# Expert lists by counting and one-hot products, one program block, and expert weights asked for by two engines

## What is computed

```
x = x + attention(norm(x), ctx, ctx) @ w_out.T             # 16 heads, causal
x = x + ffn(norm(x))                                       # dense, 1376 wide, plus LoRA experts (top 2 of 8)
x = x + softmax(norm(similarity(norm(x), ctx @ W_k.T)))    # 512 x 512 a batch
h = norm(x)
scores = softmax(h @ router_w.T)                           # 2048 tokens, 64 experts
w, idx = top_k(scores, 8); w = w / w.sum()
# every expert takes its tokens in token order, at most 128:
pos = (cumsum(onehot(idx)) * onehot(idx)).sum() - 1; valid = pos < 128
x = x + sum over its experts of w * (silu(h @ w_gate) * (h @ w_up)) @ w_down
```

## Time and profile before

| | before |
|---|---|
| median of 3 runs | 1468.0 us (1466.2 to 1468.45) |
| the profiled execution | 1466.93 us |
| its span, first to last instruction | 1465.1 us |
| TensorE busy | 1219.6 us (83%) |
| VectorE busy | 826.5 us (56%) |
| ScalarE, GpSimd busy | 498.4, 488.2 us |
| mean granted TensorE clock | 0.928 of full |
| end of the last feed-forward, of the tail, of the expert products | 1016, 1073, 1430 us |

### The profile page before, as it was taken

One profiled execution on the slowest core, in us unless ns is written; L12 is line 12 of the kernel. 1 busy time (PEld: TensorE's weight loads), 2 busy tenths in 40 slices (PEclk: granted clock), 3 DMA queues, 4 the chain that ended last, 5 costly groups with the idle time before them and its releaser, 6 DMA issues. The chain is left out here.

```text
span 1465.1 us, 19951 instructions
## 1 busy us (share of the span) xinstructions
PE 1219.6 (83%) x6297; PEld 892.1 (61%) x6297; DVE 826.5 (56%) x1677; ACT 498.4 (34%) x1137; POOL 488.2 (33%) x539
## 2 busy tenths in 40 slices
PE   0698999887899987789998788998406999999990
PEld 0566777655777765567786566776204666666660
DVE  7674777576677758577866846664582222222220
ACT  1582312565222167422127633221202323333230
POOL 3530222633022372302236230121004555555541
PEclk9998999998999999999999989999757999999995
DMA  7002221000322100042200003220078999999966
GB/s 254 1 1 93 79 97 60 1 1 30 121 84 103 52 1 1 30 135 95 97 34 0 1 32 114 103 104 0 29 318 261 349 355 342 340 358 349 292 89 130
DMA packets 44659, 180.77 MB, mean 123 GB/s; under 512 B 5356, under 2 KB 8428, under 8 KB 35764
## 3 DMA queue, kind: packets, MB, share of 16 engines
q1 hardware_dynamic: 29732, 140.15, 25.5%
q0 software_dynamic: 14864, 39.85, 12.0%
HBM read 149.28 MB, written 34.90 MB: 126 GB/s over the span
## 5 line engine op out<-in xcount | busy, mean ns | idle before, releaser
L1819 PE MATMUL PS<-WE,XGT 128*128 128x384 f32 x512 | 194.8, 504 | 1.5 <-DVE HM L1929 0.8
L682 ACT ACTIVATE P<-PS,NM 128x512 f32<-128x512 f32 (+3 forms) x256 | 132.2, 536 | 50.7 <-DVE NM L1054 49.6
L1367 PE MATMUL PS<-XTH,WHI 128*128 128x512 f32 x352 | 141.6, 402 | 1.3 <-ACT SIL L825 1.3
L811 ACT ACTIVATE WHI<-WRAW 128x1280 fp32r<-128x1280 f32 x44 | 56.1, 1274 | 248.9 <-DMA WRAW<-in_ffn 248.9
L1368 PE MATMUL PS<-XTL,WHI 128*128 128x512 f32 x352 | 139.9, 397 | 0.0
L1369 PE MATMUL PS<-XTH,WLO 128*128 128x512 f32 x352 | 139.6, 397 | 0.0
L596 POOL CAST HH<-HID 128x512 fp32r<-128x512 f32 x44 | 28.1, 639 | 328.6 <-DVE HID L1279 317.1
L1232 DVE TENSOR_TENSOR WLO<-WRAW,WHI 128x584 fp32r<-128x584 f32 (+1 forms) x88 | 110.8, 1259 | 29.4 <-ACT WHI L811 17.3
L1054 DVE TENSOR_REDUCE NM<-PS 128x2 f32<-128x1024 f32 (+2 forms) x96 | 98.7, 1042 | 48.2 <-PE PS L1376 47.6
L1819 PEld LDWEIGHTS PS<-WE,XGT 128*128 128x128 f32 x512 | 88.2, 192 | 57.9 <-issue 23.5
L1427 PE MATMUL PS<-ident,P 128*128 128x128 f32 x640 | 101.6, 297 | 23.1 <-ACT P L682 12.8
(11 more groups left out here) (273 smaller groups left out, 2768.1 us busy)
## 6 DMA issues: line engine op xcount, KB each, us to landing
WE<-in_we SPq DMA_DIRECT2D x64, 1152.0 KB, 8.2
WRAW<-in_ffn SPq DMA_DIRECT2D x44, 932.0 KB, 4.6
hx<-HN SPq DMA_DIRECT2D x4, 1152.0 KB, 4.4
acc<-HN SPq DMA_DIRECT2D x17, 256.0 KB, 4.6
XIN<-in_x SPq DMA_DIRECT2D x4, 1024.0 KB, 10.5
out<-X SPq DMA_DIRECT2D x4, 1024.0 KB, 4.2
out<-acc POOLq DMA_DIRECT2D x1, 4096.0 KB, 23.0
CTX<-in_ctx SPq DMA_DIRECT2D x4, 256.0 KB, 7.5
```

The source lines that it names most:

```text
L682: act.activation(prob(t, n), PS[:, c0:c0 + (t + 1) * P], ACT.Exp, bias=NM[:, c:c + 1], accum_out=SSUM[:, c:c + 1]).then_inc(S["p_ready"], 1)
L811: act.activation(WHI[slot][:, 0:WD], WRAW[slot][:, 0:WD], ACT.Copy).then_inc(S["wg_hi"], 1)
L1367: pe.matmul(dst, a[0], b_[0], start=first, stop=False, **kw)
L1819: mm = pe.matmul(bank(2 + s % 2, 0, 2 * F1), XGT[s % 2][:, k, :], WE[s][:, k * 2 * F1:(k + 1) * 2 * F1], start=(k == 0), stop=(k == KC - 1))
```

## The change

One part removes the keys and list rounds and makes the lists by counting:

- The position of a token in its expert's list is the count of chosen tokens ahead of it: TensorE multiplies MK with a triangular matrix (`before`) and with ones; TAKEN carries the counts of earlier batches. VectorE adds them in AT and splits the position into a high part (16 steps of 8) and a low part (8).
- For a tile of 128 tokens VectorE makes HIGH (128 x 64 x 16) and LOW (128 x 64 x 8, scaled by the token's number) by comparing with `steps_of`; TensorE multiplies them, 8 experts at a time, and the number lands at its place in the list. Two tiles share a bank; `fold` adds it to SLOTS.
- For batches 0 to 2 this runs inside ffn(b+1), in steps placed behind certain chunks of TensorE and VectorE (`list_step`, LIST_TILES). For the last batch `last_list` does it in one go, the two LOW factors scaled on ScalarE, and SPREAD brings the result to IDX's form.
- `gates` gets one more operation (two from the second list on) behind MK, on the way to the gates and to LG.
- hx is stored for the last batch in two parts, hidden columns first, gate columns when they are there.

The other part is the order of the program: one block instead of two, buffers placed so that six experts' weights are loaded during the last feed-forward and six behind it; the loops over chunks are written out on all engines; from expert 12 on SyncE asks for even experts' weights, ScalarE for odd ones, behind its copy of YE.

```diff
+LIST_TILES = (2, 3, 6, 7)
 # SyncE, feed(b)
-                with sp.Fori(1, NF // 2) as i:
-                    load_w(2 * i, 0)
-                    load_w(2 * i + 1, 1)
-                load_w(NF - 1, 0)
+                for f in range(2, NF):
+                    load_w(f, f % 2)
+                    if last and f < 8:
+                        load_expert(f - 2, f - 2)
...
+                if last:
+                    sp.wait_ge(S["ffn_ps"], 1 + NT * B)
+                    alone(sp, "sp")
+                    for e in range(6, NW):
+                        load_expert(e, e)
 # SyncE, experts
+            def reload(e, s, r):
+                if s % 2:
+                    return
 # ScalarE, expert(e, s, r)
+                expert_out(e - 1, (s - 1) % NW)
+                if s % 2 == 0 and not (isinstance(e, int) and e > E1 - NW):
+                    slot = (s - 1) % NW
+                    alone(act, "act")
+                    act.dma_start(WE[slot][:, :], w["we"][span(e - 1 + NW, P), :]).then_inc(expert_loaded[slot], 16)
 # VectorE, gates
+                step(dve.tensor_scalar(AT[:, :, :], SR[:, :, :], 0.0, FAR, ALU.is_ge, ALU.mult))
+                if b > 0:
+                    step(dve.tensor_tensor(AT[:, :, :], AT[:, :, :], TAKEN[:, :].unsqueeze(1).broadcast_to([P, NT, E1]),
+                                           ALU.add))
 # VectorE, beside ffn(b+1)
+            def list_step(b, f):
+                if f == 1:
+                    dve.wait_ge(lists_loaded, 16 * len(LISTS))
+                    positions(b, 3)
+                if f - 2 in LIST_TILES and LIST_TILES.index(f - 2) % 2:
+                    fold(b, LIST_TILES.index(f - 2) // 2)
+                if f + 1 in LIST_TILES:
+                    t = LIST_TILES.index(f + 1)
+                    if t > 1:
+                        dve.wait_ge(S["tile_ps"], 1 + NT * b + t - 1)
+                    high(t, HIGH[t % 2]).then_inc(S["high_ready"], 1)
+                    step(low_01(t, LOW01))
+                    if t > 0:
+                        dve.wait_ge(S["tile_ps"], 1 + NT * b + t)
+                    dve.tensor_scalar(LOW[:, :, :], LOW01[:, :, :], numbers[:, 1 + t % 2:2 + t % 2], None,
+                                      ALU.mult).then_inc(S["low_ready"], 1)
 # VectorE, last batch
+            def last_list():
+                b = B - 1
+                positions(b, 6)
+                for t in range(NT):
+                    low_01(t, LOW4[0][t]).then_inc(S["low_01"], 1)
+                    high(t, HIGH4[t]).then_inc(S["high_ready"], 1)
+                dve.wait_ge(S["tile_ps"], 1 + NT * B)
...
+                dve.wait_ge(S["list_ps"], 1 + 1)
 # VectorE, ffn
 chunk(2 * i + d, d % 2)
...
-                        list_round(dve, (NF // 2 - 1) * 2 * b + 2 * i + d - 1, 2 * i + d - 1)
+                        if b > 0:
+                            list_step(b - 1, 2 * i + d)
 # TensorE
+            def one_hots(bk, high, low, last):
+                for e in range(0, E1, GE):
+                    mm = pe.matmul(bank(bk, e * SB, (e + GE) * SB), high[:, e:e + GE, :].rearrange("p e a -> p (e a)"),
+                                   low[:, e:e + GE, :].rearrange("p e c -> p (e c)"), start=False, stop=last,
+                                   skip_group_check=True)
+                return mm
...
+            def list_step(b, f):
+                if f == 0:
+                    pe.wait_ge(lists_loaded, 16 * len(LISTS))
+                    pe.wait_ge(S["wxT_sb"], 1 + b + 2)
+                    positions(b, 3)
+                if f in LIST_TILES:
+                    t = LIST_TILES.index(f)
...
+                    pe.wait_ge(S["high_ready"], 1 + NT * b + t + 1)
+                    pe.wait_ge(S["low_ready"], 1 + NT * b + t + 1)
+                    one_hots(3, HIGH[t % 2], LOW, t % 2 == 1).then_inc(S["tile_ps"], 1)
 # TensorE, ffn
-                with pe.Fori(0, NF // 2) as i:
-                    for d in (1, 2):
-                        gate_up(2 * i + d, d % 2)
-                        down(2 * i + d - 1, (d + 1) % 2)
+                for f in range(NF - 1):
+                    gate_up(f + 1, (f + 1) % 2)
+                    down(f, f % 2)
+                    if b > 0:
+                        list_step(b - 1, f)
```

More of the change, by code:

```diff
@@ L110, in build @@
     zrow = sb("zrow", [1, 512], BF16)
[L111 to L115, removed]
     mhalf = sb("mhalf", [P, 8])
     IDX = sb("IDX", [P, E1], U32)
-    part3_base = place["at"]
+    before = sb("before", [P, P], BF16)
+    ones = sb("ones", [P, P], BF16)
+    steps_of = sb("steps_of", [P, SA + SB])
+    numbers = sb("numbers", [P, 3])
+    same = sb("same", [P, GE])
+    SLOTS = sb("SLOTS", [P, C])
+    TAKEN = sb("TAKEN", [P, E1])
+    AT = sb("AT", [P, NT, E1])
+    MK = sb("MK", [P, NT, E1], BF16)
+    lists_base = place["at"]
+    HIGH = [sb(f"HIGH{i}", [P, E1, SA], BF16) for i in range(2)]
+    tables_base = place["at"]
     cosw = sb("cosw", [P, NT, C])
@@ L416, in ring, with experts, call @@
                     *(turned_by(ALONE, by) - turned_by(BESIDE, by) + turned_by(BESIDE, by) * a for by in "ad"))
+    def experts(engine, body, start, stop):
+        rounds = (stop - start) // NW
+        def call(i, d):
+            body((i * NW + start + d), (start + d) % NW, i + (start + d) // NW)
+        with engine.Fori(0, rounds) as i:
+            for d in range(NW):
+                call(i, d)
+        for e in range(start + rounds * NW, stop):
+            body(e, e % NW, e // NW)
     with nc.Block() as block:
@@ L611, in two_chunks @@
                         hidden_tail(2 * i + d, d % 2)
-                        if d == 1 and isinstance(i, int) and not last:
+                        if d == 1 and i == 0 and not last:
                             front_power(b + 1, 2)
@@ L615, in two_chunks @@
                         front_q(b + 1, i)
[L616 to L618 removed]
+                for i in range(NF // 2 - 1):
                     two_chunks(i)
@@ new lines, in _ @@
+            alone(pool, "pool")
+            experts(pool, expert, NX - AHEAD, E1 - AHEAD)
+            for e in range(E1 - AHEAD, E1):
+                scatter(e, e % NX, e // NX)
+            for parity in range(2):
+                pool.wait_ge(scattered[parity], 16 * (E1 // 2))
+            pool.dma_start(out[0:NTOK, :].rearrange("(a f) c -> a (f c)", f=NT),
+                           acc[0:NTOK, :].rearrange("(a f) c -> a (f c)", f=NT),
+                           accum_op=ALU.add, max_dma_last_dim=8192).then_inc(combined, 16)
@@ L841, in ffn @@
                 chunk(0, 0, b * N1 + 1)
-                with act.Fori(0, NF // 2 - 1) as i:
+                for i in range(NF // 2 - 1):
                     for d in (1, 2):
```

489 lines of the change are left out of this document (260 added, 229 removed).

## The result

The changed kernel takes 1492.9 us (median of 4, 1490.65 to 1495.0), the one before 1467.1 us (4 runs) beside it: a ratio of 1.018, 95% interval 1.015 to 1.021. The profiled execution took 1492.02 us with a span of 1490.2, against 1466.93 and 1465.1: 25.1 us more.

The account below looks back on a forecast made before the run. TensorE was taken to bound feed-forward and expert stages, VectorE's chain the hole between them. 22.0 + 13.0 + 12.5 + 1.9 - 21.4 = +28.0 us gave 1494.9, or 1496 by the median; own range 1476 to 1509, given 1466 to 1516.

Parts of the forecast that it names:

- waits for WLO: Feed-forwards of batches two to four: VectorE held before LOW makes TensorE wait six times before gate_up, +22.0 us (20.8 to 23.5).
- clock behind them: Behind those six TensorE waits: work lost to half clock, 2.6 us per long gap, half for short, +13.0 (0 to 15.6).
- TensorE's list work: Three batches' lists: 46 products at 0.08 us plus two clears each, 4.2 us a batch, +12.5 (9.4 to 17.3).
- AT ahead of LG: Between MK and LG: the new operations on AT lengthen TensorE's wait for LG, 0.3 + 0.8 + 0.8 = +1.9 us.
- tail: Between last batch and experts: index tile 20.0 us earlier, first gather another 1.4; -21.4 us (-17.6 to -23.6).
- The hold of VectorE: Second to fourth feed-forward: VectorE idle some 10 us before LOW, released by TensorE, as a sign in the profile after.
- the MK transposes taken out: TensorE, before LXL: removing them costs nothing, since what follows waits for LXL anyway.
- (a): Rival, feed-forward: VectorE's waits do not reach TensorE, so -7 us, 1461 us; chance 0.13.
- (b): Rival, expert stage: scatters slow to 11.4 us, every expert takes 0.77 more, 49 us in all, 1545 us; chance 0.05.
- ScalarE's requests: Expert stage: weight requests behind the copy of YE stay hidden; 26 x 0.5 = 13 us if that cover went.
- Early weights: Last feed-forward: earlier expert loads give nothing beyond the tail, where the first gather gains 1.4 us without them beside it.
- Written-out loops: Loops over chunks: saved branches gain nothing, since TensorE passes its loop edge in 0.24 us, the usual spacing.

Follow-up runs that it names:

- The second experiment: Changed kernel with front_q placed ahead of list_step, so only LOW and WLO stand behind VectorE's wait: 1481.3 us, ratio 1.008 to the kernel before.
- the first experiment: Changed kernel with LOW in two buffers, scaled in place, so VectorE never waits for the previous tile's product: 1462.6 us, ratio 0.996 to the kernel before.

## Why the prediction was right, point by point

The forecast was +28.0 on the profiled execution, it came to +25.1; 1496 us was said, 1492.9 measured. The terms:

| term | predicted | measured |
|---|---|---|
| waits for WLO | 22.0 | 20.8 |
| clock behind them | 13.0 | about 9 |
| TensorE's list work | 12.5 | about 6.3 |
| AT ahead of LG | 1.9 | 1.0, and 1.9 more before LXL |
| longer half clock at the start of the third and fourth feed-forward | not seen | about 7 |
| tail | -21.4 | -20.8 |
| sum | +28.0 | about +25 |

"TensorE's list work" is here what its work in the three stages grew by, counted at full clock; the MK transposes that went are taken off.

**The waits** held in every particular: six of them, at gate_up(4) and gate_up(8) of three batches, 20.8 us against the 22.0 put together from LOW (0.35 taken, 0.35 measured), front_q and one WLO. The hold of VectorE was 11.54 us where some 10 was said. The second experiment showed the parts of it, the first one the whole.

**The clock** behind them was over-sized. The work lost behind the six was 1.7, 1.4, 1.4, 2.6, 0 and 1.7 (worked out as in the table above), 8.8 in all (9.4 in the repeated execution); I had carried 2.6 over from a wait of 3.68 us to waits of 4.1 to 4.5, and half of it to the short ones. In the two executions of the changed kernel the long waits cost 1.4 to 3.0 each; of ten waits of 1.92 us, in these two and with front_q first, six cost nothing and four 1.7. So the longer ones did cost more, but equal ones differ by a factor of two or more, and the value within 0 and 15.6 was a guess.

**TensorE's list work** is the term that was sized worst. The step that failed is the price of a product of 64 columns: put between 0.058 and 0.115, 0.08 taken, from rows whose weight loads are slower. Kernel after, TensorE's timeline, position products:

```profile
417.76 0.20 PE L1839 MATMUL PS<-MK,before 128*128 128x64 bf16 x1
...
418.06 0.28 PE L1843 MATMUL PS<-MK,ones 128*128 128x64 bf16 x4
418.18 0.49 PE L1624 MATMUL PS<-XTH,WHI 128*128 128x512 f32 x1
```

14 products from 417.76 to 418.18 are 0.030 each, and the eight one-hot products at 439.57 lie as close. 46 of them with two clears come to some 2.1 us a batch instead of 4.2. The lower end was not low enough: the weight loads of these products last 98 ns each too, as in the earlier trace rows, and follow each other at the same 0.030, so they overlap, and the length of one was no bound of the spacing.

**The longer half clock** was missed altogether. The prediction put the MK transposes taken out at nothing, because LXL is waited for anyway, and AT at its own length. Both hold as far as they go. The transposes took 0.83 us (901.02 to 901.85 in the kernel before), the wait that came for them 0.63, and with transposes put back the stages were no longer and no shorter. The operations on AT last 0.33 and 0.79 us as forecast. The wait for LG grew by 1.0 between the first two profiles, by 1.8 to 2.3 between the repeated ones (13.2 against 11.4 and 10.9), and fell by 2.4 when AT was moved. But the stretch at half clock behind them doubled, in the third and fourth batch, by 3.5 and 3.3 us in the profiled execution, and by 4.5 and 4.3 in the repeated one. This and the over-sized terms nearly cancel: the clock, the list work, the waits and AT were over by some 12 us, and 9 were missed. That the total came out within 3 us is luck; that it came out slower by about this much is not, since 20.8 of it were read correctly.

**The tail**: -20.8 for -21.4; from MK to IDX -19.9 for -20.0. Within it 1.74 a tile (1.75 said), the last 16 products 1.03 (2.0 said), OWN and its neighbours longer, the SPREAD products 3.65 (3.1 said).

**The rivals.** (a) did not come true, but the first experiment built its world, a VectorE that is not held: 1462.6 us, and (a) had said 1461. That is luck as well: (a) had 14.4 us for the products and AT. The first experiment has about 16 beside the tail, and 5.7 of them are the longer half clock, which (a) did not have. (b), slower scatters: the pace is 4.93 us an expert still, the adds land in 8.6. ScalarE's requests: nothing, as said.

**Early weights** were given 1.4 us in the tail, by the fastest gather of the trace. Against the kernel before, the first gather came out 1.0 shorter (4.8 to 3.8). But their worth in the new order is larger, 4.3 us in the first gather: 4.8 was the price of a gather sent when the loads were nearly through (424 GB/s when it was sent, 240 by 1108), not of one that flies beside them. In the new order the lists are ready sooner. With late weights the loads are asked for from 1082.39 on, the gather follows 16 us later and takes 8.0.

**What stays open.** What keeps the clock down for 12 us and more at the start of the third and fourth feed-forward. The gap before LXL is not needed for it, and it came back behind waits for LG of 3.7, 2.4 and 2.0 us, no longer than before the change. Most of these variants were profiled once, and their runs differ among themselves by as much as the effect, so no repair is shown to work. The DMA traffic of expert weights is no explanation, since the third batch has none and lost as much.

## What to carry to other kernels

Before a step is put into another engine's slack, write down what stands in the queue behind it: a wait for a buffer does not cost its length but that of everything queued between it and the next thing somebody needs, and here a second buffer, in the place of a scratch tile of the same size, was worth 30 us. Time freed on an engine that does not set the pace is worth nothing (92 us of VectorE's here, but for the hole where it did set it); the place of the new instructions in its queue decided the result. Where the clock falls after gaps, sum the work lost at half rate before and after: it is a term like any other, but with an error as large as itself. And profile a variant more than once before a clock term is put down to it.

## What the runs showed of the hardware that was not expected

- Products of 64 columns in bf16 with their own 128 x 128 weights follow each other at 0.030 us at full clock, though a single weight load lasts 98 ns. At half clock 16 of them take 1.03, 0.064 each (tail of the kernel after).
- Half clock outlasted a wait by 5.3 us or by 12.5, with TensorE busy in both, in one execution without any gap in between (windows above); in the last batch a wait of 1.92 us was followed by full clock at once, and one of 2.0 us in another place by 4.6 us of lost work.
- A gather of 128 rows takes 3.8 us to the first use of its rows when it finds quiet DMA engines, and 8.0 beside twelve weight loads.
- Written-out loops: the first batch's stage from the LoRA rows to LD takes 113.0 us, with loops of two chunks it took 112.9; in a repeated execution of each 111.4 and 111.4. The Trainium skill (Runtime: NRT & Kernel Launch, Instruction fetch mechanics) holds that a taken branch out of the prefetched pages stalls the fetch. No such stall shows here.
